# Row attention on one Trainium2 core: the two rows with the high part of a batch's maxima are issued on ScalarE's queue in every batch

## What is computed

```
projected = einsum('bte,fe->btf', query, in_proj_weight)      # q, k, v: 16 heads x 8
attention = einsum('bhtd,bhkd->bhtk', q / sqrt(8), k) + causal_mask
x = einsum('bhtk,bhkd->bhtd', softmax(attention), v)
out = einsum('bte,fe->btf', x, out_proj_weight)
x1 = layernorm(query + out)
```

## Time and profile before

| | us |
|---|---|
| median of 3 runs | 755.43 |
| lowest, highest | 755.4, 756.83 |
| the profiled execution | 757.44 |
| its span | 755.7 |
| TensorE busy in the span | 540.7 (72%) |
| VectorE | 426.2 (56%) |
| GpSimd | 393.1 (52%) |
| ScalarE | 334.1 (44%) |

### The profile page before, as it was taken

One profiled execution on the slowest core, in us unless ns is written; L12 is line 12 of the kernel. 1 busy time (PEld: TensorE's weight loads), 2 busy tenths in 40 slices (PEclk: granted clock), 3 DMA queues, 4 the chain that ended last, 5 costly groups with the idle time before them and its releaser, 6 DMA issues. The chain is left out here.

```text
span 755.7 us, 15995 instructions
## 1 busy us (share of the span) xinstructions
PE 540.7 (72%) x5471; PEld 359.4 (48%) x5473; DVE 426.2 (56%) x1106; ACT 334.1 (44%) x712; POOL 393.1 (52%) x642
## 2 busy tenths in 40 slices
PE   3769989999999626999738999999600148878300
PEld 2235555565555325999725777777400024434100
DVE  2656876878785254555417788888358831110005
ACT  1045765777767502555324666665300004443106
POOL 5244754656545404444175777773263035887634
PEclk9988998999999856999957999999755558998855
DMA  4656876767520001222221122221154011323327
GB/s 115 123 124 151 168 169 133 157 128 131 129 42 18 15 9 38 66 67 67 50 66 32 44 58 58 68 54 30 43 208 37 0 24 39 41 45 39 28 30 211
DMA packets 72950, 57.70 MB, mean 76 GB/s; under 512 B 15633, under 2 KB 62641, under 8 KB 72881
## 3 DMA queue, kind: packets, MB, share of 16 engines
q1 hardware_dynamic: 64648, 47.32, 26.9%
q0 software_dynamic: 7936, 9.07, 7.5%
q10 hardware_dynamic: 296, 0.41, 0.3%
HBM read 36.96 MB, written 19.55 MB: 75 GB/s over the span
## 5 line engine op out<-in xcount | busy, mean ns | idle before, releaser
L599 DVE TENSOR_REDUCE a_mx<-a_psR 128x6 f32<-128x768 f32 x128 | 121.9, 954 | 46.4 <-PE a_psR L322 44.6
L511 ACT ACTIVATE a_pr<-a_psR 128x768 f32<-128x768 f32 x128 | 103.5, 810 | 66.4 <-PE a_psR L335 65.6
L251 POOL TENSOR_SCALAR_AFFINE_SELECT a_pr<-a_pr 128x512 f32<-128x512 f32 x128 | 80.4, 635 | 91.3 <-ACT a_pr L511 91.1
L777 POOL DMA_INDIRECT e_xt<-x1d,source x40 | 38.2, 956 | 54.8 <-PE e_psX L788 33.7
L1659 POOL DMA_INDIRECT acc<-e_ot,ids x32 | 50.8, 1588 | 21.2 <-issue 8.5
L1651 POOL DMA_INDIRECT e_xg<-tab,ids x32 | 31.2, 976 | 50.3 <-POOLq L1373 40.9
L314 PE MATMUL a_psR<-a_maskA,identb 128*128 128x256 bf16 x256 | 53.1, 292 | 3.9 <-issue 2.8
L1018 POOL DMA_INDIRECT a_yg<-ys,slot x32 | 36.0, 1124 | 22.3 <-POOLq L732 14.9
L332 PE MATMUL a_psR<-a_qs,a_ks 50*128 50x256 bf16 x256 | 36.2, 280 | 13.3 <-DMA a_qs<-a_mlo 10.9
L1686 DVE TENSOR_TENSOR e_ot<-e_psZ,e_xg 128x512 f32<-128x512 f32 x8 | 5.5, 691 | 71.0 <-PE e_psZ L1752 36.1
L342 PE MATMUL a_psO<-a_pr,a_va 128*32 128x256 f32 x512 | 41.6, 397 | 4.5 <-ACT a_onT L503 2.8
(11 more groups left out here) (304 smaller groups left out, 1401.1 us busy)
## 6 DMA issues: line engine op xcount, KB each, us to landing
qkd<-a_hml SPq DMA_DIRECT2D x16, 384.0 KB, 4.4
fcs<-in_fc SPq DMA_DIRECT2D x16, 256.0 KB, 5.5
a_qs<-qkd SPq DMA_DIRECT2D x31, 96.0 KB
a_ks<-qkd SPq DMA_DIRECT2D x31, 96.0 KB
ys<-e_yt SPq DMA_DIRECT2D x40, 64.0 KB, 1.5
x1d<-a_x SPq DMA_DIRECT2D x16, 128.0 KB, 2.0
pjs<-in_pj SPq DMA_DIRECT2D x8, 256.0 KB, 6.0
a_x1t<-x1d SPq DMA_DIRECT2D x16, 128.0 KB
```

The costliest lines, as they stand in the source:

```text
L251: g.affine_select(out=diagonal, in_=diagonal, pattern=[[0, 4], [1, 128]], compare_op=ALU.is_ge, fill=0.0, base=0, channel_multiplier=-1).t ...
L511: a.activation(pr[s][:, :, 0:3, :].rearrange("p x k q -> p x (k q)"), psR[:, r:r + 2, 0:384], ACT.Exp).then_inc(probs, 1)
L599: v.tensor_reduce(mx[b % 2][:, :, 2 * u:2 * u + 35:17], psR[:, r:r + 2, 0:384].rearrange("p x (k c) -> p x k c", c=128), AX.X, ALU.max).th ...
L777: pool.indirect_dma_start(xt[n % 4][:], None, x1d, bass.IndirectOffsetOnAxis(ap=source[:, n:n + 1], axis=0)).then_inc(x_in[n % 4], 16)
```

## The change

In batches 1 to 15 the two rows with the high part are issued by ScalarE, behind a wait for its own cast, as batch 0 has it already. SyncE keeps the two low rows.

```diff
@@ SyncE
                 if V is not None and V >= 1:
-                    for part, ready, a in ((mhi, mhi_sb, 0), (mlo, mlo_sb, 1)):
-                        sp.wait_ge(ready, V + 1)
-                        for row_half in range(2):
-                            load_row(sp, V, part, a, row_half)
+                    sp.wait_ge(mlo_sb, V + 1)
+                    for row_half in range(2):
+                        load_row(sp, V, mlo, 1, row_half)
@@ ScalarE
                         a.copy(mhi[V % 2][:].rearrange("r x q -> r (x q)"), psM[0:2 * HP, 0:T]).then_inc(mhi_sb, 1)
+                        act.wait_ge(mhi_sb, V + 1)
+                        for x in range(2):
+                            load_row(act, V, mhi, 0, x)
                         if V == 0:
-                            act.wait_ge(mhi_sb, 1)
-                            for x in range(2):
-                                load_row(act, 0, mhi, 0, x)
                             act.wait_ge(mlo_sb, 1)
                             for x in range(2):
                                 load_row(act, 0, mlo, 1, x)
```

## The result

The changed kernel took 793.33 us (median of 4 runs, 784.78 to 797.79) beside 755.46 us for the kernel before on the same chip: a ratio of 1.0459, interval 1.0371 to 1.0547. The ratio leaves out the run of 797.79 us, which counts as slow; the two medians alone give 1.050. The side was forecast rightly, the size was not: the 13.1 us of the sum became about 38, and the time lies far above the range.

What follows compares the result with a forecast made beforehand. TensorE was taken to bound the row attention, busy 12.79 of 13.00 us a batch. Terms of 19.6 - 1.0 - 5.08 - 0.38 = +13.1 us on 755.43 gave 768.6 us, range 763 to 777 us.

Steps and rivals of the forecast that it cites:

- the 13.1 us of the sum: Whole kernel: stalls of 19.6 us less 1.0, 5.08 and 0.38 us in batches 1, 5 and 7, so 13.1 us slower.
- forecast 1.40: ScalarE between cast and onT: wait and two issues delay onT by 1.40 us in each of batches 2 to 15, 19.6 us.
- -5.08: Batch 5: the 2.43 us wait for rows and the slow clock behind it go, saving 5.08 us.
- its 0.38: Batch 7: the stage of 13.38 us loses its wait for rows, saving 0.38 us.
- the 12.7 of those terms: Stages 3 to 15: 13 stalls of 1.40 us less 5.08 and 0.38 us, 12.7 us more.
- a partly hidden stall: Rival, at onT: small waits of TensorE and ScalarE close up, leaving 1.0 us a batch; 763 us, chance 0.06.
- a faster kernel: Rival: issues cost only ScalarE's idle time, stall near zero, gains remain; 750.4 to 753.0 us, chance 0.04.
- The nearest row: Last expert stage: TensorE busy 0.12 of 1.50 us at clock 1.00, taken as evidence that idling 1.58 us costs no clock.
- a clock that falls in every batch: Rival, row attention: the clock falls in each batch at 2.65 us each; above 800 us, chance 0.03.
- -1.0: Batch 1: low rows no longer behind the high ones land earlier, saving 1.0 us.
- Rows that land earlier: Batches 1 and 5: low rows, no longer behind high ones on SyncE's queue, land 1.0 us earlier, of 1.75 possible.
- the first rival: Low rows land no earlier: batch 1 gains nothing, batch 5 still waits 0.9 us; 770.5 to 773.1 us, chance 0.22.

Runs made afterwards that it cites:

- the second profile: The changed kernel run again, unchanged, on another chip; 789.61 us against 754.82 for the kernel before, ratio 1.0445.
- The filler run: The changed kernel with TensorE's wait for onT filled by useless products of constants; 773.89 us against 754.14 for the kernel before, ratio 1.025.
- experiment 8: The changed kernel with ScalarE's wait and both issues moved behind unit 5's exponential and the x1 halves; 751.65 us against 754.82 for the kernel before, ratio 0.996.
- experiment 6: The changed kernel with ScalarE's copy of onT moved ahead of the cast and its issues; 760.56 us, ratio 1.0059 to the kernel before.
- Experiment 9: The changed kernel with high rows on ScalarE in batches 1 and 5 only, else on SyncE; 745.32 us against 746.79 for the kernel before, ratio 0.9984.
- both stalls: The kernel before with three, then four, scratch copies on ScalarE between cast and onT; 770.59 us (ratio 1.019) and 775.3 us (ratio 1.0372).

## Why the prediction was right in its side and wrong in its size

**Right, step by step.** onT came 1.37 us later (forecast 1.40). The pair of issues took 1.15 us and the gaps around it the rest (1.25 and 0.06 forecast). TensorE's wait was 1.57 us (1.58). Nothing hid it: the steady stages went from 13.0 to 14.4. Batches 5 and 7 waited for no rows, and stage 6 kept its clock, so -5.08 came as sized; stage 7 lost its 0.38 in the second profile, and fell in the first. The filler run, which is the change without its falls, has 13.1 us in stages 3 to 15 for the 12.7 of those terms. The rivals of a partly hidden stall and of a faster kernel fell.

**The step that failed** is the sentence "Here the idle 1.58 us at unit 5 has a price only if the clock falls for it. The nearest row speaks against that". The clock did fall: in five stages of the first profile, six of the second, at 1.5, 3.4 or 4.5 us each, 15.3 and about 20 us in all, and in the tail for another 5.8 us of the first profile. The row chosen as nearest was nearest in length alone: a stretch of the expert stage with TensorE idle at a clock of 1.00. The row attention had a nearer one, and the prediction used it elsewhere: batch 5's wait of 2.43 us with 0.50 behind it, in the same loop between the same products. Between 0.18 us (never a fall) and 2.43 us (one) the new 1.58 us lay open, and by both ends the term should have been 0 to 14 x 2.65 = 37 us, in the range. It was written down as a rival, "a clock that falls in every batch", with a chance of 0.03 and no case between none and all; the truth was between, 5 or 6 of 13 stages. From the sum to the profile's 34.0 us: 13.1, and 15.7 for the falls, and 6.1 for the tail (7.5 for the 1.4 forecast there), and 1.4 for batch 1 (0.4 where -1.0 was set), less 2.3 given back behind.

**Rows that land earlier: right in batch 5, wrong in batch 1, and for a further reason.** SyncE's queue shows what the prediction's rows leave out. Before, SyncE was still issuing expert weights when the cast of batch 5 began (105.90 us); in the changed kernel it was done with them before the cast (110.38 us):

```profile
105.82 0.82 SPq L1874 DMA_DIRECT2D pjs<-in_pj  x1
106.75 0.38 SPq L201 DMA_DIRECT2D qkd<-a_hml  x1
...
109.63 0.38 SPq L201 DMA_DIRECT2D qkd<-a_hml  x1
111.20 1.18 SPq L181 DMA_DIRECT2D a_qs<-a_mlo  x2
```

So the low rows were issued 0.82 us behind the cast instead of 3.03, not only the 1.75 us earlier of which 1.0 was taken. That they landed earlier is seen in experiment 8, where TensorE isn't late: 1.14 us sooner behind the cast than before, close to the 1.0. In the changed kernel both worked together, these rows and a TensorE that came 1.2 us later, at 6.92 us behind the cast. The earlier rows alone left a wait of 1.29 us (experiment 8); no run has the late TensorE with low rows as late as before. In batch 1 the low rows were issued at 50.2 us instead of 52.0, but took 6.5 to 6.8 us to land instead of 4.3 to 5.5, and unit 0 began at 57.85 us instead of 57.63: nothing of the 1.0 came. There the first rival, rows that land no earlier, was right; in batch 5 the 0.9 us of wait that it had left did not come.

**What stays open.** Why one standstill of 1.5 us brings the clock down and the next of the same length doesn't, and why some falls come at once and some 1.2 to 1.5 us later. Length isn't the whole of it: waits of 2.02 us (experiment 6, stage 6) left the clock at 1.00, 1.29 us (experiment 8, stage 6) was followed by 0.89. The runs show that more stages fall as the standstill grows, not the rule. That the clock is the larger share of the tail's growth is read from the two profiles of the changed kernel, not tested; with the filler the tail was 28.5 us too, so more than the standstill at onT bears on it.

## What to carry to other kernels

Before a DMA issue or a wait is put on a compute engine's queue, look at who waits for the next instruction behind it: the same two issues cost 1.4 us a batch directly behind the cast and nothing behind three more activations. Price a new standstill of TensorE twice, for its length and for the clock behind it; where the loop's own trace shows a fall after a longer wait and none after a shorter, the new one's clock price has both as bounds, and a row from another stage doesn't close them. A cheap test is a filler: if the time falls when the wait is stuffed with useless products, the clock was the price. And when small transfers are late, look for what shares the DMA engines with them, rather than for another queue.

## What the runs showed of the hardware

- How often the clock falls rises steeply with the length of the standstill, in stages with 12.8 us of TensorE's work: falls in 0 of 13 stages with waits of 0.93 us, in 2 with 1.42, in 5 with 1.52, in 5 and 6 with 1.57 (one profile each, two with 1.57, not all on the same chip). Each fall began within 1.6 us after TensorE resumed. The Trainium skill, page "TensorE: Matmul & The Clock Gate", section "A second HAM failure mode: psum-queue depth-cycling", tells of a kernel whose TensorE idles briefly between groups often enough that its clock swings; the traces here agree. Experiment 9 adds a fall after a single standstill of 1.58 us.
- ScalarE begins to issue a transfer while its earlier instructions still compute: at 173.90, 0.35 us before the end of an exponential and ahead of two further activations in program order. Directly behind a wait for the engine's own last result the pair cost 1.40 us a stage instead of nothing.
- Falls come in fixed sizes: stages of 14.4 us become 15.9, 17.8 or 18.9 to 19.1 us, in the changed kernel and in both stalls; stages of 13.8 to 14.2 us become 15.5 to 15.8.
